# Stack loads by quarters of an image in the attention phase, and the last result chunk in four stores

## The reference

```
y = layernorm(x1).reshape(B, C, H, W)          # C = 24, H = W = 64
y = depthwise3x3(conv1x1(pin_w, y))            # 126 channels
x2 = x1 + conv1x1(pout_w, gelu(y[:, :63]) * y[:, 63:])
```

## Time and profile before

| what | value |
|---|---|
| time, median of 3 runs | 233.79 us (231.95 to 235.48) |
| the profiled execution: its own time, and its span | 230.8 us, 228.9 us |
| granted clock over the span | 0.993 |
| PE busy | 210.9 us (92%) |
| DVE, ACT, POOL busy | 159.3, 137.0, 127.1 us |
| transfers | 12541 packets, 25.09 MB |

### The profile page before, as it was taken

One profiled execution on the slowest core, in us unless ns is written; L12 is line 12 of the kernel. 1 busy time (PEld: TensorE's weight loads), 2 busy tenths in 40 slices (PEclk: granted clock), 3 DMA queues, 4 the chain that ended last, 5 costly groups with the idle time before them and its releaser, 6 DMA issues.

```text
span 228.9 us, 8584 instructions
## 1 busy us (share of the span) xinstructions
PE 210.9 (92%) x3634; PEld 109.6 (48%) x3634; DVE 159.3 (70%) x284; ACT 137.0 (60%) x226; POOL 127.1 (56%) x165
## 2 busy tenths in 40 slices
PE   7779899999999999997799999999999987999980
PEld 4346666676757667665455444443333311222240
DVE  4677969698997989798755756344368789655332
ACT  3567676777859686763236333333346774898980
POOL 8245948466988869695989993223320000245433
PEclk9999999999999999999999999999999999999997
DMA  6950000120130464665637367777400001243312
GB/s 159 307 148 3 3 3 9 37 72 3 39 74 22 106 228 132 200 215 160 196 84 253 113 244 183 232 235 271 153 4 0 4 0 33 64 114 94 82 37 69
DMA packets 12541, 25.09 MB, mean 110 GB/s; under 512 B 6618, under 2 KB 8162, under 8 KB 10775
## 3 DMA queue, kind: packets, MB, share of 16 engines
q1 hardware_dynamic: 11606, 23.16, 33.6%
q0 software_dynamic: 896, 1.38, 2.7%
HBM read 18.63 MB, written 3.15 MB: 95 GB/s over the span
## 4 chain that ended last, share of the span: by engine, by line
PE 82%; DVE 7%; issue 4%; POOL 2%; ACT 2%; DMA 1%; POOLq 0%; DVEq 0%
PE psum L668 13%; PE psum L669 12%; PE psum L613 10%; PE psum L624 7%; PE psum L642 7%; PE psum L859 4%; PE psum L659 4%; PE psum L573 3%; PE psum L839 3%; PE psum L569 3%; PE psum L817 3%; PE psum L830 2%; PE psum L596 2%; PE psum L580 2%; PE psum L588 2%
## 5 line engine op out<-in xcount | busy, mean ns | idle before, releaser
L505 POOL TENSOR_TENSOR diff<-biased,mx 128x768 f32<-128x768 f32 x31 | 45.7, 1475 | 22.7 <-DVE mx L1146 22.7
L1277 DVE TENSOR_TENSOR gated<-psum,gel 64x512 f32<-64x512 f32 x32 | 22.1, 693 | 24.5 <-ACT gel L1030 24.5
L324 POOL DMA_DIRECT2D out<-yo x28 | 14.2, 515 | 44.2 <-DVE yo L1379 44.2
L1142 DVE TENSOR_TENSOR biased<-psum,pk 128x768 f32<-128x768 f32 x31 | 29.5, 952 | 11.2 <-PE psum L613 10.9
L1030 ACT ACTIVATE gel<-psum 64x512 f32<-64x512 f32 x32 | 18.9, 591 | 30.7 <-PE psum L669 30.6
L954 ACT ACTIVATE pt<-psum 128x768 f32<-128x768 f32 x32 | 25.9, 810 | 16.6 <-PE psum L624 16.4
L668 PE MATMUL psum<-sta,pk 108*128 108x512 f32 x64 | 33.7, 608 | 0.5 <-issue 0.5
L669 PE MATMUL psum<-stb,pk 108*128 108x512 f32 x64 | 32.7, 592 | 0.0
L1146 DVE TENSOR_REDUCE mx<-biased 128x12 f32<-128x768 f32 x31 | 29.5, 953 | 1.1
L613 PE MATMUL psum<-kmv,stq 32*64 32x192 f32 x512 | 28.1, 334 | 0.4 <-DVE biased L1154 0.3
L642 PEld LDWEIGHTS psum<-val,pt 128*32 128x32 f32 x1536 | 17.1, 110 | 12.4 <-issue 12.2
(11 more groups left out here) (108 smaller groups left out, 343.9 us busy)
## 6 DMA issues: line engine op xcount, KB each, us to landing
sta<-scratch SPq DMA_DIRECT2D x24, 288.0 KB
stb<-scratch SPq DMA_DIRECT2D x24, 288.0 KB
xtok<-xt SPq DMA_DIRECT2D x8, 192.0 KB, 4.2
xin<-xw SPq DMA_DIRECT2D x8, 192.0 KB, 5.5
x<-x1s SPq DMA_DIRECT2D x28, 48.0 KB
out<-yo POOLq DMA_DIRECT2D x28, 48.0 KB, 2.0
pk<-pack SPq DMA_DIRECT2D x1, 827.5 KB, 7.1
scratch<-ytok SPq DMA_DIRECT2D x4, 192.0 KB, 3.9
```

The source lines that it names most:

```text
L505: g.tensor_tensor(diff[:, t % 2].rearrange("q g w n -> q (g w) n"), scores_of, mx[:, t % 2].unsqueeze(2).to_broadcast([128, 4 * NH, WT]), ...
L1142: v.tensor_tensor(biased[:, slot].rearrange("q (p s) -> q p s", p=2), banks, wt("rpb").unsqueeze(1).to_broadcast([128, 2, 2 * NH * WT]), A ...
L1277: v.tensor_tensor(gated[64 * (b % 2):64 * (b % 2) + 64, b // 2, c * CH:(c + 1) * CH], bank(u % 4)[64:128], gel[:, u % 4, :], ALU.mult).the ...
```

## The change

The row of a stack load becomes one piece instead of two. `parts_of(b, h)` gives 2 for both halves of image 0 and for the first half of image 1, and 1 for the other five halves. With 2 parts, the half is loaded in two quarters of the image: first the six transfers of one quarter (both stacks, three taps), then the six of the other, each of 36 rows of 4 KB. With 1 part it is six transfers of 36 rows of 8 KB. The wait in `edges` is for 96 instead of 48 where there are 2 parts; what it guards is still the whole half. `store_last` goes: SP stores chunk 7 in four transfers of whole rows (2 KB), behind the second of DVE's two halves, and waits for half as large a count. The access pattern on both sides is otherwise unchanged, as are the orders of SP, POOL and PE.

```diff
-        def load_stack(queue, b, h, paced=False):
-
-            half = NT // 2
-            for n in range(2):
-                c0, c1 = STACKS[n]
-                for y in range(3):
...
-                    src = bass.AP(src.tensor, src.offset + off, [[NT, c1 - c0], [1, 3], [half // 2, 2], [1, half // 2]])
-                    dst = stack(n, b)[y:RS:3, half * h:half * h + half].rearrange("p (q n) -> p q n", q=2)
-                    queue.dma_start(dst, src).then_inc(stack_in[n][b][h], 16)
+        def parts_of(b, h):
+
+            return 2 if 2 * b + h < 3 else 1
+
+        def load_stack(queue, b, h):
+
+            parts = parts_of(b, h)
+            cols = NT // 2 // parts
+            for part in range(parts):
+                at = NT // 2 * h + cols * part
+                for n in range(2):
+                    c0, c1 = STACKS[n]
+                    for y in range(3):
+                        src = scratch[b]
+                        off = PAD + (y - 1) * W - 1 + c0 * NT + at
+                        src = bass.AP(src.tensor, src.offset + off, [[NT, c1 - c0], [1, 3], [1, cols]])
+                        queue.dma_start(stack(n, b)[y:RS:3, at:at + cols], src).then_inc(stack_in[n][b][h], 16)
...
-            queue.wait_ge(yo_ready, c + 1)
+            queue.wait_ge(yo_ready, c + 1 if c < NCH - 1 else NCH + 1)
...
-        def store_last(queue, half, images, done):
...
-            for half in range(2):
-                store_last(sp, half, range(B), last_stored)
-            sp.wait_ge(last_stored, 32 * B)
+            store_result(sp, NCH - 1, range(B), last_stored)
+            sp.wait_ge(last_stored, 16 * B)
...
-                    pool.wait_ge(stack_in[n][b][h], 48)
+                    pool.wait_ge(stack_in[n][b][h], 48 * parts_of(b, h))
```

More of the change, by code:

```diff
@@ L398, in _ @@
                     wait_for_y(b)
-                    load_stack(sp, b, 0, False)
+                    load_stack(sp, b, 0)
                 if m in (5, 7):
-                    load_stack(sp, m // 2 - 2, 1, False)
+                    load_stack(sp, m // 2 - 2, 1)
             store_y(sp, 5)
```

## The result

| | before | after |
|---|---|---|
| median of 5 runs each | 232.74 us | 239.59 us |
| ratio of the runs | | 1.0307, 95% interval 1.0218 to 1.0395 |
| the profiled execution: its own time, its span | 230.8, 228.9 us | 238.84, 237.1 us |
| granted clock over the span | 0.993 | 0.981 |

The change is slower by 3.1%. The forecast was 235.5 us, in a range of 230 to 240. It had the sign and the place, at a quarter of the size: +1.7 us on the median, where +6.9 came.

The account below looks back on a forecast made before the run. PE was taken as the bound (82% of the wait chain), with SP timing the late stack loads. 230.8 + 4.2 (SP) - 1.0 (end) = 234.0 us; between that and 237.0, 235.5 us was taken, range 230 to 240.

Parts of the forecast that it names:

- the rivals: Three alternatives: stalls gone, SP punctual (226.9 us, chance 0.15); only the end counts (229.8, 0.15); lateness plus clock (238.2, 0.2).
- The whole halves: Five unsplit half loads: both pieces of a row already travel as one 8 KB packet, so 0.
- SP's lateness: 18 added stack issues of 0.79 us delay SP's load of image 2 by 4.2 us (3.0 to 5.7), costing +4.2 us.
- the first step: Load of image 0 half 0 on SP: takes 9.5 us instead of 4.76 and ends at 87.4 us.
- PE at chunk 24: End of the convolutions: borders of chunks 20 and 24 end at 157.2 and 165.0 us, PE starting chunk 24 0.1 us later.
- The sign named for it: Profile after: idle PE of 3 us or more ahead of chunk 20 or 24, released by POOL's border.
- The slower rival: SP late plus PE's clock halved after idling at chunk 20: 238.2 us, 241.2 on the median; chance 0.2.
- The fetch stalls: PE's two instruction stalls in attention step 6, 2.9 us: shrinking them is worth 0 under SP's lateness, otherwise up to 2.9.
- The view that 4 KB rows would end them: Rival: smaller packets let instruction blocks in sooner and SP isn't late; 226.9 us, 229.9 on the median; chance 0.15.
- The end: Last stores: SP's four whole stores replace eight, POOL's last store landing at 227.3 us bounds the gain; -1.0 us (0 to 1.6).
- The rule on initiating transfers: Skill page: initiating is usually small beside the DMA, making 18 issues cost about 0; weighed against the trace's 0.746 us, rejected.
- The middle between profile and median: Profiled execution is 3.0 us under the median; whether this hides or adds gives 234.0 or 237.0; 235.5 us taken.

Follow-up runs that it names:

- experiment 1: Changed kernel with all eight halves whole (6 issues each), new end kept: ratio 1.0046 to the kernel before, span 230.1 us.
- experiment 12: Changed stacks with the end of the kernel before (eight half stores): ratio 1.0242 to the kernel before.
- experiment 5: Changed kernel, SP issuing the x1 rows of step 5 ahead of the load of image 1 half 0: ratio 1.0329 to the kernel before.
- experiment 6: Changed kernel, SP issuing the token store of step 5 ahead of the load of image 1 half 1: ratio 1.0142 to the kernel before.
- experiment 4: Changed kernel with only image 1 half 0 quartered (6 added issues), new end: ratio 1.0138 to the kernel before.
- experiment 2: Kernel before plus 18 dummy issues of 576 bytes, six behind each of the first three half loads: ratio 1.0272, span 234.4 us.
- experiment 3: Changed kernel with quarters for image 0 only (12 added issues), new end: ratio 1.0055 to the kernel before.
- experiment 8: Kernel before, with the token store of step 5 ahead of the load of image 1 half 1: ratio 0.9995.
- experiment 11: Whole-half kernel with token store first and chunk 6 stored by ACT (0.9908), given the change's quarters and earlier x1 rows: ratio 0.9994 to the kernel before.

## Why the prediction was right and wrong

**The range: held, in part by luck.** 239.59 us is 0.4 us inside 230 to 240. Without the rivals the range ended at 238.5; the rest was there for a half clock at chunk 20, which did not come. What filled it was for the most part SP's larger lateness. On the profiled execution the sum was 234.0 us and 238.84 came: 2.3 us more from SP, 1.4 of scatter and 1.3 at the end, which is the difference within 0.2 us.

**The whole halves: right.** 0 was forecast; experiment 1 has 1.0046, with an interval of 0.9999 to 1.0094, the new end included.

**SP's lateness: the mechanism right, the size too small.** The lateness at image 2's load was put at 4.2 us (3.0 to 5.7) and measured 6.5. The price of an issue was right: a median of 0.746 to 0.751 us for all 66 and nothing for the smaller row. So was the first step (87.4 forecast, 87.2 measured). What was too small is the share of long issues. 18 issues of 0.79 us less the 8.6 us of gaps are 5.6 us; 4.2 came out because I put the 2.2 us issue of image 1 half 0 back to an ordinary one, and kept a long one only as the far bound. After the change, three came in the same stretch: 1.25 us at 87.28, one of 1.22 within the 2.80 at 98.66, and 1.99 at 104.43, 2.6 us above ordinary ones together. With SP's slack gone, each comes through to the end; the 2.2 us one before had 2.3 us of idle SP behind it. The three runs with 18 added issues and SP's old order stand at 6.0 to 6.6 us, all above 5.6.

**PE at chunk 24: right in place.** The borders were to end at 157.2 and 165.0 us and did at 160.1 and 168.7. Of the 3.7 us by which the second is later, 2.3 are SP's and 1.4 the scatter of experiment 12. The sign named for it, 3 us or more of idle PE, came in two pieces, 2.1 us ahead of chunk 20 and 1.5 ahead of chunk 24.

**Who waits for the rows: missed.** I moved `store_x1(5)` by 4 us and more in the sum and did not say that DVE writes the next rows into its buffer. It cost PE 3.2 us and a stretch at half clock. It hides behind chunk 20 in the change (experiment 5) and comes out when that is mended (experiment 6). The slower rival had the half clock from an idle PE, at chunk 20; it came at the rows instead and did not set the end.

**The fetch stalls: worth nothing, but not for the reason of size.** They were costed at 0 behind SP, and that held. The view that 4 KB rows would end them did not: with 8 KB rows they are 1.56 and 1.35 us before, and one of 0.22 in experiment 1; with a quartered half 2.43 us in experiment 4. They come at the same instructions and change with the execution: with image 1 half 0 whole they stand in three of seven profiles, with it quartered in one of seven, too few to say that the row size has no part. Without them PE waits for POOL at the next step, so 2.9 us of stall were worth 1.5 us at most: chunk 0 starts at 111.29 after and at 112.76 before.

**The end: wrong.** -1.0 was forecast, +0.3 came. SP's side did come 0.6 us earlier. But I took 227.3 us, the landing of POOL's last store, as POOL's end; its drain ran to 228.7 before, and after the change, at 5.3 us behind the start of DVE's last instructions, it ended last.

**The rule on initiating transfers** that I weighed (the Trainium skill, "DMA: Bandwidth & Descriptors", "Issuing engines are not separate DMA queues"), that initiating is usually short beside the transfer itself, did not hold on this full queue: 0.77 us to initiate 576 bytes (0.80 with the step), and 18 of these cost 2.7% of the whole time in experiment 2.

**The middle between profile and median: a wrong guess.** What varies between executions is also the start: in the profiles of experiments 1, 3, 4 and 8 the clock stands at 0.50 to 0.53 from 9.4 to 12.6 us, and the first stack load comes at 79.3 to 80.9 us; in the other ten it stands at 1.00, and the load comes at 77.8 to 78.1. That shifts SP with everything else and is not hidden by its lateness. By the mechanism, the choice on top, 237.0, was the better one.

Open: what makes a single issue long; and how much of the 0.9% in experiment 11 is SP's slack, how much the moved rows and how much chance, since the two versions were not measured side by side; and why POOL's drain is 0.2 us longer with the new end (3.84 to 3.87 us in the change and experiments 1 and 4, 3.62 to 3.63 before and in experiment 12).

## What to carry to other kernels

An engine that only issues transfers has a budget like any other, and the page's busy shares leave it out: list its gaps, and count an added issue at its full time once they are used up, long issues included. Here splitting a transfer cost by the issue, not by the byte; and where a queue waits for a small store behind a large load, swap the two first. When one late queue feeds two waits in a row, mending the first alone can show nothing, as in experiment 5.

## What was not expected of the hardware

An issue on SP took 0.75 to 0.77 us (medians) whether it carried 288 KB, 144 KB or 576 bytes to 36 rows, and single ones took up to 2.2 us. In the change the clock stood at 0.50 for 6.8 us (125.6 to 132.4), PE being idle from 123.7 to 126.9. The length of such a gap alone does not tell whether the clock falls: behind the 2.12 us of idle at chunk 20 it stayed at 1.00, behind 2.08 us in experiment 2 and 2.14 us in experiment 12, at 124 to 126 us, it stood at 0.50. POOL's drain behind its last four stores took 3.6 to 3.9 us, and each of these spans ended 0.2 to 0.3 us behind its end.
